# Four whole-row transfers in place of sixteen small ones for each block move of a four-layer graph-attention kernel

## What is computed

```
q, k, v = (x @ Wq + bq), (x @ Wk + bk), (x @ Wv + bv)     # 8 heads of 64
scores  = leaky_relu(q k^T / 8 + edge_bias[adj])          # 1024 x 1024 for each head
attn    = softmax(where(adj > 0, scores, -1e9))
out     = concat_heads(attn @ v) @ Wp + bp
```

## Time and profile before

| | |
|---|---|
| median of 3 runs | 9005.03 us |
| lowest, highest | 9004.63, 9019.0 us |
| span of the profiled execution | 9019.7 us |
| PE, DVE, ACT busy | 8145.7, 7407.4, 7012.7 us |
| mean granted TensorE clock | 0.959 |

### The profile page before, as it was taken

The page is one execution under the profiler, slowest core; times in us unless marked ns, Lnnn a source line. Parts: engine busy times, 40 slices in busy tenths (PEclk is TensorE's granted clock), DMA queues, the critical chain, the costliest instruction groups (busy, mean ns, idle before and its releaser), DMA issues.

```text
span 9019.7 us, 165963 instructions
## 1 busy us (share of the span) xinstructions
PE 8145.7 (90%) x58360; PEld 3645.7 (40%) x58360; DVE 7407.4 (82%) x11189; ACT 7012.7 (78%) x8204; POOL 1428.7 (16%) x582
## 2 busy tenths in 40 slices
PE   3899998989999999998999989999899998989999
PEld 1534435344353433434334353443534435343352
DVE  3788787988879878798787978878788787988878
ACT  2787786977869778797787878778687786977877
POOL 0301203021030301203012030120302103021000
PEclk7999999999999999999999999999999999999999
DMA  2714426253262623526245271442615426253251
GB/s 73 159 35 107 107 52 156 42 124 87 61 143 51 141 63 71 135 48 157 44 91 122 43 171 36 103 109 54 156 39 115 98 52 152 46 129 77 60 123 19
DMA packets 2150362, 822.71 MB, mean 91 GB/s; under 512 B 1146914, under 2 KB 2129954, under 8 KB 2147362
## 3 DMA queue, kind: packets, MB, share of 16 engines
q1 hardware_dynamic: 2149410, 810.76, 40.5%
HBM read 76.25 MB, written 4.19 MB: 9 GB/s over the span
## 4 chain that ended last, share of the span: by engine, by line
PE 38%; SPq 23%; DVE 15%; issue 13%; ACT 9%; DMA 1%; DVEq 0%; POOL 0%; ACTq 0%; POOLq 0%
SPq L381 22%; PE psum L817 21%; DVE work L1400 6%; ACT work L1043 5%; PE psum L528 3%; PE psum L600 3%; PE psum L695 2%; DVE work L1279 2%; PE psum L670 1%; DVE work L1251 1%; PE psum L523 1%; PE psum L545 1%; ACT spare L886 1%; ACT spare L881 1%; PE psum L784 1%
## 5 line engine op out<-in xcount | busy, mean ns | idle before, releaser
L817 PE MATMUL psum<-work,pick 128*32 128x512 f32 x32768 | 3766.7, 599 | 192.1 <-DVE work L1400 161.5
L1043 ACT ACTIVATE work<-spare,ucol 128x1024 f32<-128x1024 f32 x3402 | 3631.8, 1145 | 51.9 <-PE psum L817 47.3
L1400 DVE TENSOR_SCALAR work<-spare,ucol 128x1024 f32<-128x1024 f32 x4790 | 3248.9, 744 | 72.3 <-PE psum L817 55.9
L817 PEld LDWEIGHTS psum<-work,pick 128*32 128x32 f32 x32768 | 977.8, 110 | 2531.4 <-issue 2069.1
L953 ACT ACTIVATE work<-psum,beta 128x1024 f32<-128x1024 f32 x1024 | 1139.6, 1113 | 559.8 <-PE psum L670 398.5
L1251 DVE CUSTOM_DVE_ANT_0 work<-psum,work 128x1024 f32<-128x1024 f32 x1024 | 1227.0, 1198 | 247.1 <-ACT work L953 237.4
L1279 DVE STREAM_TRANSPOSE work<-work 128x1024 f32<-128x1024 f32 x960 | 1190.9, 1240 | 263.3 <-DMA work<-work 168.7
L960 ACT ACTIVATE work<-work,least 128x1024 f32<-128x1024 f32 x1024 | 1172.7, 1145 | 27.5 <-DVE least L1251 27.5
L1481 POOL TENSOR_TENSOR rstd<-rstd,neg_half 128x8 f32<-128x8 f32 x64 | 131.6, 2056 | 5024.0 <-DVE rstd L1190 5024.0
L670 PE MATMUL psum<-x_split,q_hi 128*128 128x512 f32 x2048 | 852.2, 497 | 0.0
L666 PE MATMUL psum<-mask,ident_b 128*128 128x512 bf16 x2048 | 636.7, 393 | 228.3 <-DVE least L1251 225.1
(11 more groups left out here) (167 smaller groups left out, 7053.2 us busy)
## 6 DMA issues: line engine op xcount, KB each, us to landing
work<-work SPq DMA_DIRECT2D x2560, 128.0 KB, 2.4
spare<-work SPq DMA_DIRECT2D x1280, 128.0 KB, 2.5
adj_in<-in_adj SPq DMA_DIRECT2D x128, 512.0 KB, 4.8
q_lo<-adj_in SPq DMA_DIRECT2D x1024, 64.0 KB, 2.1
q_lo<-spare SPq DMA_DIRECT2D x1024, 64.0 KB, 2.1
work<-work SPq DMA_DIRECT2D x1792, 32.0 KB, 1.9
mask<-mask_next SPq DMA_DIRECT2D x16, 2048.0 KB, 9.2
x_in<-in_x SPq DMA_DIRECT2D x16, 256.0 KB, 10.2
```

Of the source, the lines that this page charges most:

```text
L817: mm = pe.matmul(slot[32 * q:32 * q + 32, cols], pick[:, 15 - kk:47 - kk], ring[kk % 4][q][:, cols], start=False, stop=(kk == 15), skip_gr ...
L1043: ins = act.activation(ring[kk % 4][q], v3, ACT.Relu, bias=ucol[:, 4 * T + q, kk:kk + 1])
L1400: ins = dve.tensor_scalar(ring[kk % 4][q], v3, ucol[:, 4 * T + q, kk:kk + 1], 0.0, ALU.add, ALU.max)
```

## The change

Each move is 4 transfers in place of 16. Transfer a reads the whole source quadrant a (32 partitions, each with all of its row) and writes one slot a of all 128 destination partitions. The elements are taken in order, so source partition p, part c of its row, lands in destination partition 4p + c. For this to be key 4p + c of its group of 128, part c of a source row has to hold the keys 4j + c: the transposes now read every fourth column (`by_part`), so that turned row j of part c is key 4j + c. The `blocks` tiles are laid out with part c outermost, the destination tiles with source quadrant a outermost, and the reads of the products follow. A contiguous run of a transfer is now 4 KB for a quad, 2 KB for a pair and 1 KB for a tile, where it was 512, 256 and 128 bytes. The sum of bytes is the same. The number of instructions on PE, DVE, ACT and POOL is the same, the order on every queue too.

```diff
+MOVE_DONE = 4 * 16
+def by_part(rows):
+
+    return rows.rearrange("p (b j c) -> p c b j", c=4, j=32)
             def move(dst, src, done):
-                for turn_ in range(4):
-                    for a in range(4):
-                        c = (a + turn_) % 4
-                        sp.dma_start(dst[32 * c:32 * c + 32, :, a, :], src[32 * a:32 * a + 32, :, c, :]).then_inc(done, 16)
+                for a in (0, 2, 1, 3):
+                    sp.dma_start(dst[:, a, :], src[32 * a:32 * a + 32]).then_inc(done, 16)
...
-                    src = blocks[k % 2].rearrange("p (b c x) -> p b c x", c=4, x=P)
-                    dst = quadT[k % 3].rearrange("p (b c x) -> p b c x", c=4, x=P)
+                    dst = quadT[k % 3].rearrange("p (a y) -> p a y", a=4)
-                    move(dst, src, s_moved[k % 4])
+                    move(dst, blocks[k % 2], s_moved[k % 4])
...
-                move(pairA_T.rearrange("p (b c x) -> p b c x", c=4, x=F),
-                     blocksA[m % 2].rearrange("p (b c x) -> p b c x", c=4, x=F), s_moved_a)
+                move(pairA_T.rearrange("p (a y) -> p a y", a=4), blocksA[m % 2], s_moved_a)
...
-                move(tile3T.rearrange("p (b c x) -> p b c x", c=4, x=32),
-                     blocks3.rearrange("p (b c x) -> p b c x", c=4, x=32), s_moved3)
+                move(tile3T.rearrange("p (a y) -> p a y", a=4), blocks3, s_moved3)
...
-                pe.wait_ge(s_moved_a, (g * NT + m + 1) * 256)
-                src = pairA_T.rearrange("p (b a t i) -> p b a t i", a=4, t=2, i=32)
+                pe.wait_ge(s_moved_a, (g * NT + m + 1) * MOVE_DONE)
+                src = pairA_T.rearrange("p (a b t i) -> p b a t i", a=4, t=2, i=32)
...
-                src = quadT[k % 3].rearrange("p (b a h x) -> p b a h x", a=4, h=2, x=F)
+                src = quadT[k % 3].rearrange("p (a b h x) -> p b a h x", a=4, h=2, x=F)
...
+                src = tile3T.rearrange("p (a b i) -> p b a i", a=4, i=32)
                 for j in range(NT):
                     half = slice(F * (j % 2), F * (j % 2) + F)
-                    mm = pe.matmul(outT[half, T % 4 * P:(T % 4 + 1) * P], values[3][:, j, :],
-                                   tile3T[:, j * P:(j + 1) * P], start=(j < 2), stop=(j >= NT - 2))
+                    dst = outT[half, T % 4 * P:(T % 4 + 1) * P].rearrange("p (a i) -> p a i", a=4)
+                    mm = pe.matmul(dst, values[3][:, j, :], src[:, j, :, :], start=(j < 2), stop=(j >= NT - 2))
                 mm.then_inc(s_pv3, 1)
...
-                dst = blocksA[m // 2 % 2].rearrange("p (b t i) -> p b t i", t=2, i=32)
-                dve.transpose(dst[:, :, m % 2, :], probsA.rearrange("p (b j) -> p b j", j=32))\
+                dst = blocksA[m // 2 % 2].rearrange("p (c b t i) -> p c b t i", c=4, t=2, i=32)
+                dve.transpose(dst[:, :, :, m % 2, :], by_part(probsA))\
                    .then_inc(s_blocks_a, 1)
...
-                    dst = blocks[k % 2].rearrange("p (b h t i) -> p b h t i", h=2, t=2, i=32)
-                    dve.transpose(dst[:, :, h, half, :], probs[n % 4].rearrange("p (b j) -> p b j", j=32))\
+                    dst = blocks[k % 2].rearrange("p (c b h t i) -> p c b h t i", c=4, h=2, t=2, i=32)
+                    dve.transpose(dst[:, :, :, h, half, :], by_part(probs[n % 4]))\
...
-                dve.transpose(blocks3.rearrange("p (b i) -> p b i", i=32),
-                              probs3[T % 2].rearrange("p (b j) -> p b j", j=32)).then_inc(s_blocks3, 1)
+                dve.transpose(blocks3.rearrange("p (c b i) -> p c b i", c=4, i=32), by_part(probs3[T % 2]))\
+                   .then_inc(s_blocks3, 1)
             def copy_tile3(it):
                 filled(dve, it, ("tile3", 0))
-                dve.tensor_copy(tile3T, turn).then_inc(s_turn_free, 1)
+                dve.tensor_copy(tile3T.rearrange("p (a b i) -> p b a i", a=4, i=32),
+                                turn.rearrange("p (b a i) -> p b a i", a=4, i=32)).then_inc(s_turn_free, 1)
```

More of the change, by code:

```diff
@@ L377, in move @@
             def move(dst, src, done):
-                for turn_ in range(4):
-                    for a in range(4):
-                        c = (a + turn_) % 4
-                        sp.dma_start(dst[32 * c:32 * c + 32, :, a, :], src[32 * a:32 * a + 32, :, c, :]).then_inc(done, 16)
+                for a in (0, 2, 1, 3):
+                    sp.dma_start(dst[:, a, :], src[32 * a:32 * a + 32]).then_inc(done, 16)
             def move_quads(g, more, tail):
-                ready(s_moved_a, (g * NT + NT) * 256)
+                ready(s_moved_a, (g * NT + NT) * MOVE_DONE)
                 if more:
@@ L688, in pv_quad @@
                         pe.wait_ge(s_beta4, g + 1)
-                    pe.wait_ge(s_moved[k % 4], g * (MOVES[k % 4] * 256) + (moved_before(k) + 1) * 256)
-                src = quadT[k % 3].rearrange("p (b a h x) -> p b a h x", a=4, h=2, x=F)
+                    pe.wait_ge(s_moved[k % 4], g * (MOVES[k % 4] * MOVE_DONE) + (moved_before(k) + 1) * MOVE_DONE)
+                src = quadT[k % 3].rearrange("p (a b h x) -> p b a h x", a=4, h=2, x=F)
                 cols = slice(2 * tt * P, 2 * tt * P + 2 * P)
@@ L828, in layer3 @@
                     if T and kk == 14:
-                        pe.wait_ge(s_moved3, (g * (NT - 1) + T) * 256)
+                        pe.wait_ge(s_moved3, (g * (NT - 1) + T) * MOVE_DONE)
                         pv_tile(g, T - 1)
@@ L1158, in blocks_a @@
                 if m % 2 == 0 and (m >= 4 or not_first(g)):
-                    dve.wait_ge(s_moved_a, (g * NT + m // 2 - 1) * 256)
+                    dve.wait_ge(s_moved_a, (g * NT + m // 2 - 1) * MOVE_DONE)
                 dve.wait_ge(s_probs_a, g * 2 * NT + m + 1)
-                dst = blocksA[m // 2 % 2].rearrange("p (b t i) -> p b t i", t=2, i=32)
-                dve.transpose(dst[:, :, m % 2, :], probsA.rearrange("p (b j) -> p b j", j=32))\
+                dst = blocksA[m // 2 % 2].rearrange("p (c b t i) -> p c b t i", c=4, t=2, i=32)
+                dve.transpose(dst[:, :, :, m % 2, :], by_part(probsA))\
                    .then_inc(s_blocks_a, 1)
@@ L1274, in turn_tile @@
                     dve.wait_ge(s_moved[(k - 2) % 4],
-                                g * (MOVES[(k - 2) % 4] * 256) + (moved_before(k - 2) + 1) * 256)
+                                g * (MOVES[(k - 2) % 4] * MOVE_DONE) + (moved_before(k - 2) + 1) * MOVE_DONE)
                 if moved:
                     dve.wait_ge(s_probs, g * TILES2 + n + 1)
-                    dst = blocks[k % 2].rearrange("p (b h t i) -> p b h t i", h=2, t=2, i=32)
-                    dve.transpose(dst[:, :, h, half, :], probs[n % 4].rearrange("p (b j) -> p b j", j=32))\
+                    dst = blocks[k % 2].rearrange("p (c b h t i) -> p c b h t i", c=4, h=2, t=2, i=32)
+                    dve.transpose(dst[:, :, :, h, half, :], by_part(probs[n % 4]))\
                        .then_inc(s_blocks, 1)
@@ L1352, in blocks_tile3 @@
                 if T:
-                    dve.wait_ge(s_moved3, (g * (NT - 1) + T) * 256)
+                    dve.wait_ge(s_moved3, (g * (NT - 1) + T) * MOVE_DONE)
                 dve.wait_ge(s_probs3, g * NT + T + 1)
-                dve.transpose(blocks3.rearrange("p (b i) -> p b i", i=32),
-                              probs3[T % 2].rearrange("p (b j) -> p b j", j=32)).then_inc(s_blocks3, 1)
+                dve.transpose(blocks3.rearrange("p (c b i) -> p c b i", c=4, i=32), by_part(probs3[T % 2]))\
+                   .then_inc(s_blocks3, 1)
             def copy_tile3(it):
                 filled(dve, it, ("tile3", 0))
-                dve.tensor_copy(tile3T, turn).then_inc(s_turn_free, 1)
+                dve.tensor_copy(tile3T.rearrange("p (a b i) -> p b a i", a=4, i=32),
+                                turn.rearrange("p (b a i) -> p b a i", a=4, i=32)).then_inc(s_turn_free, 1)
             def out3(g, it):
```

## The result

| | before | after |
|---|---|---|
| median | 9008.75 us (4 runs, 9004.63 to 9019.0) | 9536.19 us (4 runs, 9533.42 to 9549.31) |
| ratio | | 1.0584 [1.057, 1.0597] |
| span of the profiled execution | 9019.7 us | 9531.3 us |

The change made the kernel 5.8% slower. The page shows in its first lines which engine did it: busy time by engine, and the chain by engine and line, against the earlier trace rows.

What follows compares the result with a forecast made beforehand. The prediction took SP's issue of transfers to bound the layer 2 stage. From 9019.7 us it took 141 for the groups and 40 before the first, giving 8839, less 14.7 for the median: 8825 us, range 8750 to 9400.

Steps and rivals of the forecast that it cites:

- SP's issue: Layer 2 stage: issuing transfers on SP sets the pace, 11.79 us a quad; the change takes it off the path.
- A move's issue: SP queue: issuing a move falls from 10.5 us to 1.5, each new transfer costing 0.36 us like the adj load.
- The data: Layer 2 moves: 2 MB per quad take 9.4 us at 222 GB/s; a move lands about 12 us after its start.
- The steady stretch: Layer 2, 12 quads a group: from 11.79 to 11.2 us a quad, 7.1 us a group.
- the tail: End of the layer 2 stage: PE's last wait for a move, 1.71 us a group, goes too.
- Before the first group: Layers 0 and 1 alone: eight moves of a pair save 5.4 us each, 43, partly covered, so 40 us.
- PE's reads and the copies: PE's product reads, bounds 0 to -0.2 us per product, and the copy L1360: no change taken for either.
- The transposes: All 83 of a group, reading SBUF strided: between no cost and 1.06 us longer each; no cost taken, 57%.
- Half pace: Rival, 21%: strided transposes take 1.06 us longer, DVE bounds layer 2 at 14.2 us a quad, median 9820 us.
- No faster transfers: Rival, 8%: DMA engines are the limit, 2 MB take 11 us or more, period stays 11.8 us; 8965 to 9005 us.
- the likeliest case: Whole kernel with strides free, 57%: 8825 us, with 8750 to 8920 us as its own range.
- What would show it: Signs in the profile: L1279 mean 1240 ns or 2300, DVE's move waits under 100 us, DMA packets below 0.3 million.

## Why the prediction was wrong, point by point

- **SP's issue bounds the layer 2 stage, and the change takes it off the path.** Right: SPq fell from 22% to 2% of the chain, and without the stride the kernel gains 1.3%.
- **A move's issue falls to 1.5 us.** Wrong: 6.8 to 8.1 us. The estimate took the adj load's 0.36 us, which stood behind transfers of 128 KB; behind four of 512 KB the same load takes 1.50. In a run of four the first two take 0.6 us each, the third 4.2 and the fourth 2.7. Alone on the chip it is the same (0.68, 0.64, 4.37 and 2.39), so no other traffic is needed for it. What the third one waits for no row names.
- **The data take 9.4 us and a move lands after 12.** Too low: 12.9 us alone, over 13 in the kernel. Alone the four transfers move 162 GB/s over their whole time and the 16 of before 170, not the 222 that I took from one stretch. That one transfer reads one quadrant I named as a reason to keep the old rate, and in the last rival, but gave it no price; the transfers that read all partitions bound it, 6.88 us against 12.91, together with the change of partition.
- **The steady stretch goes to 11.2 us a quad, 141 us in all with the tail.** Without the stride it goes to 11.36 to 11.41 in the group read here. Over all 16 groups 12 quads take 137.16 us on average instead of 141.12: 4.0 x 16 = 63 us for the forecast 113. Of the tail's 27 us some 10 came: PE waits 47 us for `spare` where it waited 66.5, and from quad 14's move to the first move of layer 3's stage it is 68.5 us on average instead of 69.1. What remains of DVE's waits, 196 us where I said under 100, comes of the late landing, since the halved move takes them to 0.0.
- **Before the first group, 40 us.** Right: 5.1 us less from one pair to the next for the forecast 5.4, and that in the changed kernel, with its slower transposes. Without the stride layer 2's first transpose starts at 233.1 us where it started at 269.8, 37 us earlier. With the 63 and the 10 above that is 110 of the 129 us by which the span without the stride (8890.8) is under that of before; forecast 181. The other 19 are not placed.
- **PE's reads and the copies cost nothing.** Right: PE L696 393 ns for the 394 of L695 before, the product of layer 3 280 ns for 288, the copy 1221 for 1220.
- **The transposes at the lower end of their bounds.** This is the step that failed. I took "no cost" from the only strided row, L1169, which reads PSUM. The price is 0.84 us a transpose of layer 2 and 0.9 to 1.0 of the others, over 1328 transposes. The stride of L1169 was even sixteen times wider, and this made it look like the harder case; but it was another memory, and the kernel that reads PSUM strided shows that the row was right for PSUM and said nothing of SBUF. The Trainium skill's Advanced Engine Details and Errata, section Memory Cachelines, warned of just this, and the runs agree with its 16 bytes: step 2 is free, step 3 in between, steps 4 and 8 the same.
- **Half pace, 21%: 9820 us.** This rival had the mechanism, and is 284 us too high. Its transpose was 1.06 us longer and is 0.84; its quad was 14.2 us and is 13.15. The layer 3 stage it priced at 12 us a group, measured 13.5. 9536 lies above the range, which took in a cost of up to 0.65 us. The 21% for this rival was by itself more than the 2 in 10 that the range was meant to leave out.
- **No faster transfers.** The four take 12.9 - 2.4 = 10.5 us for the data, between the 9.4 I took and the 11 of this rival; what the transfers gain without the stride, 120 to 139 us, lies between its 0 to 40 and the forecast 181 as well.
- **The sums.** The lower end of the likeliest case's range is 9019.7 - 229 - 40 - 14.7 = 8736 by its own terms, not 8750. Nothing hangs on it.
- **What would show it.** L1281 at 2084 ns: nearer to the 2300 than to the 1240. DVE's waits for moves did fall under 100 us, to 16, but for the other reason: a slower DVE comes later to them. DMA packets 337783, above the 0.3 million. The new transfers' median to landing is 7.7 us, under the 11 that was to be a sign of being wrong; the other sign, a transpose longer by over 0.4 us, came.

In one sum, per group against before, with the quads of the one group read above: steady stretch (13.15 - 11.79) x 12 = +16.3 us, everything else, with the gain ahead of the first group in it, +15.7: 32.0 x 16 = 512 us, the 9531.3 - 9019.7 of the spans. The same from the other side: transfers without the stride -129 (8890.8 - 9019.7), the stride on top of them +640 (9531.3 - 8890.8).

## What to carry to other kernels

Price a strided read by the memory it reads and by the 16 bytes it opens, and if the layout needs the stride, put it where an engine reads PSUM anyway. Before transfers are merged, ask which partitions each one reads: four large ones from one quadrant each landed no sooner than sixteen small ones, and after the merge a cut into eight, the first four sent early, gained about as much again (108 us, where the merge had gained 120 to 139). When an edit has a cheap part and an open part, a run that does each alone is worth more than any argument from a neighbouring row.

## What the runs showed of the hardware

- SBUF reads by DVE (transpose, tensor_tensor, tensor_reduce): 1.76 ns per 16 bytes opened, visible from a step of 3 floats on. A tensor_copy takes 0.69 us dense, 1.07 reading at step 4 and 1.10 writing at step 4. ACT pays more: 1.06 us for 1024 floats dense, 2.06 at step 4, reading or writing. PSUM at the same step: nothing, on either engine (1199 ns for 1198, 1112 for 1113).
- 2 MB from SBUF to SBUF: 6.88 us when each transfer reads all partitions, 12.91 when each reads one quadrant, 13.92 in the quadrants' natural order. In the kernel that order cost 130 us.
- A 512 KB transfer takes 0.54 to 0.68 us to issue into an empty queue, and so does the second behind it; the third in a row took 4.2 us in the kernel and 4.4 alone on the chip, the fourth 2.7 and 2.4.
